# Order of ScalarE's copies in the attention steps, record copies on another engine, and regions filled ahead

## The reference

```
x = x + layernorm(attention(layernorm(x)))      16 heads of 64, causal softmax, output projection,
                                                residual, layernorm with gamma and beta
x = x + layernorm(experts(layernorm(x)))        router softmax over 8 experts, the best 2 of them,
                                                gate_e * (gelu(x @ w1[e]) @ w2[e]) summed
```

## Time and profile before

| | us |
|---|---|
| median of 3 runs | 707.59 (707.39 to 709.84) |
| the profiled execution | 707.34 |
| its span, first to last instruction | 705.6 |
| TensorE busy | 677.8 (96%) |
| ScalarE busy | 552.3 (78%) |
| VectorE busy | 547.0 (78%) |
| GpSimd busy | 281.6 (40%) |

### The profile page before, as it was taken

How to read it: one execution, slowest core, us unless ns; L and a number is a source line. 1 busy time by engine, 2 the same in 40 slices (tenths; PEclk the granted TensorE clock), 3 DMA queues, 4 the chain that set the end, 5 groups by cost and what they waited for, 6 DMA issues and landing times.

```text
span 705.6 us, 18101 instructions
## 1 busy us (share of the span) xinstructions
PE 677.8 (96%) x5762; PEld 576.4 (82%) x5763; DVE 547.0 (78%) x2557; ACT 552.3 (78%) x1815; POOL 281.6 (40%) x424
## 2 busy tenths in 40 slices
PE   6999999999999999999999999999989999999994
PEld 5788878888878888788888788888878999999951
DVE  5677798989899898989898888888897774444326
ACT  5888888889898888888898988888885664555515
POOL 3012234343434353432323231423213777755545
PEclk9999999999999999999999999999999999999998
DMA  7900000000000000000000000000020243322155
GB/s 170 280 9 9 9 9 25 16 25 9 25 9 25 8 26 14 19 25 17 25 8 24 10 24 9 24 13 14 22 66 27 70 118 113 104 76 76 51 196 181
DMA packets 40537, 34.89 MB, mean 49 GB/s; under 512 B 10528, under 2 KB 36128, under 8 KB 40448
## 3 DMA queue, kind: packets, MB, share of 16 engines
q1 hardware_dynamic: 34816, 23.81, 12.5%
q0 software_dynamic: 4544, 9.45, 3.8%
q10 hardware_dynamic: 1088, 0.54, 0.3%
HBM read 20.22 MB, written 13.56 MB: 48 GB/s over the span
## 4 chain that ended last, share of the span: by engine, by line
PE 70%; ACT 20%; DMA 3%; DVE 2%; issue 2%; POOL 1%; DVEq 0%; SPq 0%; POOLq 0%; ACTq 0%
PE PT1O L446 13%; PE SC L434 9%; PE M L704 9%; PE M L411 6%; ACT qk L1308 5%; ACT pT L1328 5%; ACT prob L1319 5%; PE M L413 4%; PE M L412 4%; PE SC L437 4%; PE A L457 4%; ACT pT L1325 3%; PE PT1O L465 3%; PE SC L411 3%; PE SC L412 2%; PE SC L413 2%
## 5 line engine op out<-in xcount | busy, mean ns | idle before, releaser
L808 DVE CUSTOM_DVE_ANT_0 SC<-SC,mask 128x128 f32<-128x128 f32 (+1 forms) x512 | 166.0, 385 | 3.8 <-PE SC L437 3.3
L1319 ACT ACTIVATE prob<-SC,nmax 128x256 f32<-128x256 f32 x256 | 135.6, 530 | 0.0
L1308 ACT ACTIVATE qk<-M 128x512 f32<-128x512 f32 x127 | 77.6, 611 | 54.7 <-PE M L413 54.7
L446 PEld LDWEIGHTS PT1O<-pT,v_sb 128*64 128x64 f32 x1024 | 63.4, 136 | 49.1 <-ACT pT L1328 30.5
L1313 ACT ACTIVATE prob<-SC,nmax 128x128 f32<-128x128 f32 x256 | 101.9, 420 | 1.5 <-DVE nmax L808 1.5
L446 PE MATMUL PT1O<-pT,v_sb 128*64 128x256 f32 (+1 forms) x1024 | 97.3, 332 | 5.2 <-ACT pT L1328 0.9
L820 DVE TENSOR_TENSOR prob<-prob,rden 128x512 f32<-128x512 f32 x128 | 89.7, 700 | 2.4
L1610 POOL DMA_INDIRECT expert_rows<-v_sb,got x74 | 73.2, 990 | 36.2 <-ACT v_sb L1470 17.5
L1599 POOL DMA_INDIRECT sent_rows<-rec,slot x64 | 64.8, 1013 | 51.3 <-DVE slot L1074 34.9
L434 PE MATMUL SC<-qk 64*128 64x256 f32 x512 | 83.5, 403 | 0.9 <-ACT prob L1319 0.6
L411 PE MATMUL M<-xt_hi,wqk_hi 128*128 128x256 f32 x254 | 83.2, 328 | 1.2 <-ACT v_sb L1332 0.8
(11 more groups left out here) (212 smaller groups left out, 1731.3 us busy)
## 6 DMA issues: line engine op xcount, KB each, us to landing
got<-sent_rows SPq DMA_DIRECT2D x39, 132.0 KB, 2.3
w_in<-expert_rows SPq DMA_DIRECT2D x8, 512.0 KB, 4.9
x_in<-L_attn_x SPq DMA_DIRECT2D x16, 128.0 KB, 2.1
w_in<-L_ffn_w SPq DMA_DIRECT2D x1, 2048.0 KB, 12.4
x_res<-L_attn_x SPq DMA_DIRECT2D x16, 128.0 KB, 2.1
w_sb<-L_ffn_w SPq DMA_DIRECT2D x8, 256.0 KB, 4.6
out<-prob SPq DMA_DIRECT2D x6, 256.0 KB, 2.1
sent_rows<-pad_rec SPq DMA_DIRECT2D x11, 132.0 KB, 4.8
```

The lines of the kernel that those rows point to most:

```text
L446: last = mm(PT1O[k * E:(k + 1) * E, cols], v_sb[:, t, h * E:(h + 1) * E], src[:, par, k, :], start=(t == 0), stop=(t == 1), skip_group_che ...
L808: last = v.tensor_tensor_reduce(SC[par][:, k, cols], SC[par][:, k, cols], m, -1.0, -MASKED, ALU.add, ALU.min, nmax[:, par, late, k:k + 1])
L1308: a.activation(qk[:, p % 2], src[:].rearrange("p (i s) -> p i s", i=2), ACT.Copy).then_inc(qk_sb, 1)
L1319: return a.activation(prob[:, slot, k, 1:3, :].rearrange("p n t -> p (n t)"), SC[par][:, k, LATE_Q], ACT.Exp, scale=-1.0, bias=nmax[:, par ...
```

## The change

ScalarE's step is reordered: the copies of pair p-2's transposes follow the first q/k copy directly, the copies of pair p-1's transposes follow the second q/k copy directly, and both late exponentials of pair p's heads come behind them. In the first 14 batches GpSimd makes the record copies (the last two stay on ScalarE). The pad stores behind the last rows go. In their place SP fills the regions in the attention, 256 rows of all eight experts with one DMA, 16 such DMAs, each ahead of the scatter that may write into these rows. A tile's rows are read with two neighbouring rows in one partition, where they were 128 rows apart.

```diff
+        FILLED = [[], [], [0], [1, 2], [3, 4]] + [[b] for b in range(5, B)]
...
+                for j in FILLED[b] if b < B else ():
+                    if j == 0:
+                        sp.wait_ge(sem("pad_ok"), 2)
+                    else:
+                        sp.wait_ge(sem("fill_st"), 16 * j)
+                    sp.dma_start(regions[:, j * ROWS:(j + 1) * ROWS, :].rearrange("e (p t) c -> p e (t c)", p=P),
+                                 pad_rec[:].rearrange("p e t c -> p e (t c)"))\
+                        .then_inc(sem("fill_st"), 16)
...
-                    sp.dma_start(got[:, k], sent[bass.ds(rows[k], ROWS), :].rearrange("(t p) c -> p t c", p=P))\
+                    sp.dma_start(got[:, k], sent[bass.ds(rows[k], ROWS), :].rearrange("(p t) c -> p t c", p=P))\
...
-            pads()
-            sp.wait_ge(sem("pad_st"), 16 * NE)
...  ScalarE, step(b, u)
-                exps_early(p, 0)
+
                 if k == 0:
+                    exps_early(p, 0)
                     v_copy(1, 0, 0)
-                if k >= 1:
+                else:
                     pT_copies(p - 2)
-                exps_late(p, 0)
+                    exps_early(p, 0)
                 if more:
                     qk_copy(p + 3)
-                exps_late(p, 1)
                 if k >= 1:
                     pT_copies(p - 1)
+                exps_late(p, 0)
+                exps_late(p, 1)
                 exps_early(p, 1).then_inc(exp_done, 1)
                 exps_early(p + 1, 0)
...
-                if u == 2 and there(b, 2):
-                    records(b - 2)
...
-                    if n == 10:
-                        pads[:] = pad_rows()
-                        store_pads(NE // 2, 3 * NE // 4)
-                    if n == 11:
-                        store_pads(3 * NE // 4, NE)
...  GpSimd
+                pool.wait_ge(sem("fill_st"), 16 * (r + 1))
                 q.sem_inc(sem("send_turn"), 1)
...
+            def records(r):
+                pool.wait_ge(sem("xf_done"), r + 1)
+                if r:
+                    pool.wait_ge(sem("sent_st"), 16 * K * T * r)
+                for k in range(K):
+                    last = q.tensor_copy(rec[k][:, :, 0:D], xf[:])
+                last.then_inc(sem("rec_ok"), 1)
...
                     tail(b - 1, lambda: split_w1(b, 2))
+                    if there(b, 2):
+                        records(b - 2)
                     tail_end(b - 1, lambda: split_w1(b, 3))
```

More of the change, by code:

```diff
@@ L55, in sandwich_kernel @@
     back = nc.dram_tensor("expert_rows", (K * N + (NE + UNUSED) * ROWS, D), F32, kind="Internal").ap()
+    regions = sent[0:NE * CAP, :].rearrange("(e c) d -> e c d", e=NE)
     back_groups = back[0:K * N, :].rearrange("(g p r k) d -> g p r k d", g=NG, p=P, r=K)
@@ L171, in sandwich_kernel @@
         row_of = sb("row_of", [1, TILES], I32)
-        pad_row = sb("pad_row", [1, NE], I32)
         got = sb("got", [P, RING, 2, REC])
@@ L221, in sandwich_kernel @@
         LAG = 2
+        FILLED = [[], [], [0], [1, 2], [3, 4]] + [[b] for b in range(5, B)]
+        assert sum(FILLED, []) == list(range(N // ROWS))
         STEPS = NP // 2
@@ L308, in expert_weights @@
                         rows = sent[NE * CAP + k * ROWS:NE * CAP + (k + 1) * ROWS, :]
-                        sp.dma_start(rows.rearrange("(t p) c -> p t c", p=P), pad_rec[:, k])\
+                        sp.dma_start(rows.rearrange("(p t) c -> p t c", p=P), pad_rec[:, k])\
                             .then_inc(sem("spare_st"), 16)
@@ L321, in batch @@
                     sp.dma_start(x_res[:], x_tiles[b - 1]).then_inc(sem("x_res_ld"), 16)
-                if isinstance(b, int) and b < 2:
+                if b < 2:
                     expert_weights(b)
+                for j in FILLED[b] if b < B else ():
[6 more added lines that the diff above has]
+                        .then_inc(sem("fill_st"), 16)
             def table_values(row, largest, why):
@@ L1066, in find_places @@
                 dve.drain()
-                if is_last(r):
-                    v.tensor_copy(pad_row[:], base[0:1, :]).then_inc(sem("pads_known"), 1)
                 v.tensor_reduce(slot_f[:], picked[:], AX_X, ALU.add)
@@ L1433, in between @@
                     records(B - 1)
[L1435 to L1447, removed]
             def gelu(n, s, halves=range(2)):
@@ L1640, in batch @@
             def batch(b):
-                if isinstance(b, int) and b == LAG + 1:
+                if b == 2:
                     pool.wait_ge(sem("spare_st"), 16 * UNUSED)
```

## The result

The changed kernel takes 712.59 us (median of 4 runs, 712.11 to 713.08). The kernel before, run beside it, takes 708.32 (707.39 to 709.84). The ratio is 1.0065, with a 95% interval of 1.0049 to 1.0081: slower by 4.3 us. The measured time lies inside the stated 700.5 to 716.5 and just above the narrower 707.5 to 712.5: the direction was right, the size about half of what came.

A forecast was written before the change was run, and what follows sets the result against it. Predicted bound: in common attention steps, the second scores' wait for ScalarE's last exponentials. 707.34 + 3.7 - 1.5 + 0.8 + 0.7 - 1.5 = 709.5, or 709.8 as median; range 700.5 to 716.5, narrower 707.5 to 712.5.

The forecast's parts named there:

- The reordered step: Attention steps u = 0, 2, 3: 0.08 us longer each, second scores wait for exponentials; 46 steps, +3.7 us.
- Records: Two GpSimd copies in u = 2 of 14 batches delay VectorE's normalising, mostly absorbed: +0.7 us, bounds 0 and +9.
- the lock of the rival: SBUF port rule: VectorE's normalising in u = 2 may be held for a whole GpSimd record copy, or both; chance 0.2.
- rival C: Attention: delays of VectorE's normalising delay all exponentials and the scores; record copies add 4 to 9 us, 714 to 719; chance 0.2.
- Steps u = 1: Attention steps with the next batch's transposes: second transposes start earlier, -0.10 us in each of 15, -1.5 us.
- the margin of 0.10: In u = 1, how much earlier VectorE's normalising lets the second transposes start: 0.32 - 0.16 - 0.06 = 0.10 us.
- The late tile: Feed-forward stage: without pad stores SP loads earlier, so TensorE's 1.47 us stall at the first late tile goes: -1.5 us.
- Rival D: Feed-forward stage: the fills do not hide or the stall stays, +1.5 us, 711.3; no separate chance given.
- The last step: End of the attention, no q/k copies: two late exponentials queue behind the transposes copies, +0.8 us, bounds 0 and +1.
- Fills: Sixteen 1.08 MB DMAs on SP's queue in the attention, some 6.5 us each, cost 0, bounds 0 and +1.
- Rival A: Common attention steps: exponentials end by 5.7 and don't hold the scores; 0.37 us shorter each, 689 to 698; chance 0.16.
- the gate: In an attention step, second scores may not start before all exponentials of that bank's old scores end: 5.83, forecast 6.07.

The follow-up runs named there:

- the order alone: The kernel before with only ScalarE's new order (records on ScalarE, pad stores, no fills): 713.51 us, ratio 1.0068.
- fills alone: The changed kernel with the old ScalarE order and the record copies back on ScalarE: 707.53 us, ratio 0.9991.
- order undone: The changed kernel with ScalarE's old order put back, nothing else: 708.04 us, ratio 0.9992.
- filled gap: The changed kernel with the first head's late exponential moved between the early one and the second q/k copy: 701.54 us, ratio 0.9901.

## Why the prediction was near, and where it was off

**The reordered step: right, the sum with luck.** Gap of ScalarE, start of the second copy, end of the exponentials, new wait and the 1.86 behind it all came as worked out. Copy to copy, as the forecast counts, the 46 steps give +3.5 with the order alone, against +3.7. But 42 of them add up to 2.4 (0.04 to 0.07 each, not 0.08), and 1.1 comes from four that the forecast didn't see: u = 0 of batches 5 and 15, u = 3 of batch 5 and u = 2 of batch 15, 0.2 to 0.4 longer, where the second transposes wait for VectorE's normalising and all exponentials stand behind their copies. In the changed kernel the 46 steps have +4.9; GpSimd's record copies make the difference.

**Records: right in size, by another way.** Forecast +0.7, measured +1.3 (attention +4.2 against +2.9 with the order alone). Two copies of 128x256 took 0.73 together, under my 0.45 each:

```profile
327.56 0.73 POOL L1613 COPY rec<-xf 128x256 f32<-128x256 f32 x2
```

The normalising of u = 2 starts at 328.23, when they are all but over (328.29), and takes its 0.69; so the lock of the rival wasn't put to the test there. They cost in the next step, u = 3, of batches 3 to 8. That all exponentials inherit a delay of VectorE is rival C's mechanism, and it did act: it cost 1.3 us by the w1 split, about 0.9 in the four steps above (over what the others show), and at most 1.3 by the copies, which the rival had at 4 to 9.

**Steps u = 1: right in quiet batches, wrong in six.** Forecast -1.5, measured -0.7, copy to copy. In batches 9 to 14 a step is 0.08 shorter and its second transposes 0.11 earlier, against a forecast of 0.10; batches 0 to 2 give -0.9 together. In batches 3 to 8 a step is 0.14 longer, +0.8 together. The part that failed is the margin of 0.10: I took it from one quiet step (batch 9) and took no account of what GpSimd does in six other batches. L1063 was in the trace, held for 0.26 to 0.27 in them.

**The late tile: wrong.** Forecast -1.5, measured +0.3 in the profiled execution. The step that failed is "with the pads gone SP can start up to 1.77 earlier". I checked the waits in front of the loop but not the one in it, for the buffer. I had named that a removed stall needs the next-latest releaser, and looked for it among SP's waits alone. The wait for the buffer lets the load go 2.39 behind tile 8's scatter, in the changed kernel as with fills alone, order undone and filled gap. In those three the load takes 2.0 to 2.1 and the stall is 0.50, 0.37 and 0.48 (in the four kernels with pads 1.47, 1.90, 2.03 and 2.13). So some 1.0 of the forecast's 1.5 at that tile did come without the pads. The changed kernel's profiled execution shows 1.73 since its load took 3.38. In the three others it is the next tile's load that is slow (3.27, 3.77, 3.65), and what is left of the gain over both tiles is 0.7, 0.2 and 0.3. Why one load in this stretch is slow stays open. Rival D had the stall remain, at +1.5.

**The last step: right**, +0.8 forecast, +0.7 measured. **The first step: missed**, +0.5: there, too, a late exponential now stands behind the second q/k copy, with no transposes to gain from. The step behind it, u = 1 of batch 0, is 0.4 shorter and gives most of it back; this is half of the -0.9 above.

**Fills: right**, nothing in the attention. I had allowed 6.5 us for one of 1.08 MB; they landed in 5.0. The row of DMA issues of the kernel after:

```profile
sent_rows<-pad_rec SPq DMA_DIRECT2D x16, 1056.0 KB, 5.0
```

**The sum.** On the profiled execution 709.5 was forecast and 713.1 measured: +1.8 for the late tile, +0.8 for u = 1, +0.5 for the first step, +0.5 for the 46 steps and the records together, and small rests. The median lay 0.5 under the profiled run.

**Rival A** (the gate doesn't hold, 689 to 698) fell, as the 46 waits show. Its gain was real, though: it takes an order that keeps the gate at 5.83.

## What to carry to other kernels

When copies are moved ahead of other work in an in-order queue, compute when the queue's last product is due as well as the first: a gap opened in the queue (0.24 us here, in 46 steps) is paid by whoever needs the last one. Look then for one item that fits the gap; that turned +4.3 us into -6.8. And when a stall is to go, list every wait of the released engine, buffer reuse in loops too, with the time at which each is satisfied, and check a margin in a busy stage as well as in a quiet one. Count the steps of the result from the same event as in the forecast: here the other count made a gain of u = 1 look like none.

## What was unexpected of the hardware

- From a group of scores that is held for ScalarE's exponentials it takes 1.87 us to the next copy and not 1.77, and this is no single case: it is 1.86 behind 19.19, 1.87 behind 329.65, and 1.87 in the filled-gap kernel, where the wait is too short to be listed. In u = 3 of batches 3 to 8 there, where the scores start later (6.03 and more into the step instead of 5.88), it is 1.76 to 1.78.
- A VectorE operation with two SBUF inputs, 0.168 us by itself, took 0.36 beside GpSimd's 0.46 us tensor_tensor on w1, and ended with it to 0.01 us. The Trainium skill, SBUF — State Buffer, section "Who interferes with whom", says that whoever issues first holds the shared ports for its whole instruction; this trace agrees as to the order (GpSimd began at 214.93, VectorE at 215.04), and VectorE's takes 0.17 again once GpSimd starts later. That the two end together, and not one behind the other, the rule doesn't say.
- 16 writes of 1.08 MB beside the attention, 17 MB in all, changed none of its steps (0.01 us in the sum of 62).
- In two executions TensorE had stood still for 2.13 and 2.03 us at the late tile, and its granted clock then fell from 1.00 to 0.50 (2.4 to 1.2 GHz) for 3.4 us. Each time that cost some 1.5 us more than the stall: the next tile took 5.05 and 4.97 instead of 3.47. Behind the stalls of 1.90, 1.73 and 1.47 the clock stayed at 1.00.
- One chip session made every kernel 4 to 6% slower, with TensorE, VectorE and ScalarE idle together for up to 7 us while GpSimd went on. What held them is not shown.
